# Half value products in 16-head attention units, and a GpSimd chain that begins one state later in a state-space pass

## What is computed

```
v = (x @ Wv.T).reshape(B, S, H, dk).transpose(0, 2, 1, 3)
...
scores = jnp.einsum('bhqd,bhkd->bhqk', q, k) / jnp.sqrt(jnp.float32(dk))
```

```
dt = jax.nn.softplus(jnp.einsum('blr,dr->bld', dt, dt_w) + dt_b)
...
dA = jnp.exp(dt[..., None] * A)
dBx = dt[..., None] * Bc[:, :, None, :] * xs[..., None]
def step(h, inp):
    h = dA_t * h + dBx_t
    y = jnp.einsum('bds,bs->bd', h, C_t)
```

## Time and profile before

| | before |
|---|---|
| median of 3 runs (lowest, highest) | 7721.05 us (7704.44, 7728.39) |
| profiled execution, its own time | 7713.37 us |
| its span, granted TensorE clock | 7711.6 us, 0.942 |
| PE busy | 6731.2 us, 87% |
| DVE busy | 5364.4 us, 70% |
| ACT busy | 4156.1 us, 54% |
| POOL busy | 2878.0 us, 37% |
| a0, c0, f2, c3: time of a unit | 10.5, 9.67, 9.4, 9.67 us |
| a1: time of a unit | 7.62 us, or 9.1 with a fall of the clock |
| m1 and m2: time of a group | 58.6 to 63 us |

### The profile page before, as it was taken

One profiled execution on the slowest core, in us unless ns is written; L12 is line 12 of the kernel. 1 busy time (PEld: TensorE's weight loads), 2 busy tenths in 40 slices (PEclk: granted clock), 3 DMA queues, 4 the chain that ended last, 5 costly groups with the idle time before them and its releaser, 6 DMA issues. The chain is left out here.

```text
span 7711.6 us, 190413 instructions
## 1 busy us (share of the span) xinstructions
PE 6731.2 (87%) x75040; PEld 4112.0 (53%) x75040; DVE 5364.4 (70%) x8861; ACT 4156.1 (54%) x6107; POOL 2878.0 (37%) x1663
## 2 busy tenths in 40 slices
PE   7989994877777899988898868989889999989898
PEld 5766683443442333333333335667557666767676
DVE  7867465454536999988999954668667777767544
ACT  4555333454535777767777764546444444446433
POOL 3311163332312888867888810136112221211000
PEclk9999996999978999998999989999999999999999
DMA  0000001000001222212222200000000000000000
GB/s 27 0 18 14 2 0 17 2 3 2 3 8 35 71 72 76 75 54 75 71 71 77 72 9 16 11 7 0 3 29 2 2 2 2 2 13 14 14 0 22
DMA packets 117005, 191.55 MB, mean 25 GB/s; under 512 B 39542, under 2 KB 75420, under 8 KB 116060
## 3 DMA queue, kind: packets, MB, share of 16 engines
q1 hardware_dynamic: 116572, 185.25, 7.6%
HBM read 174.99 MB, written 8.09 MB: 24 GB/s over the span
## 5 line engine op out<-in xcount | busy, mean ns | idle before, releaser
L2461 POOL TENSOR_TENSOR m_dBx<-m_dtx,m_Bs 128x1024 f32<-128x1024 f32 x518 | 1212.0, 2357 | 212.3 <-DVE m_hs L2798 170.0
L2798 DVE TENSOR_TENSOR_SCAN m_hs<-m_ps_dA,m_dBx 128x512 f32<-128x512 f32 x1036 | 1207.0, 1206 | 84.0 <-POOL m_dBx L2461 82.1
L2577 PE MATMUL m_ps_y<-m_yc,ident 128*128 128x512 f32 x2072 | 1068.3, 640 | 0.0
L2670 ACT ACTIVATE m_ps_dA<-m_dt,m_A 128x504 f32<-128x504 f32 x1036 | 687.0, 678 | 485.0 <-DVE m_hs L2798 482.3
L1998 POOL TENSOR_TENSOR a_s<-a_s,a_den 128x1024 f32<-128x1024 f32 x128 | 243.7, 1904 | 1141.7 <-DVE a_den L2044 1141.7
L2809 DVE TENSOR_TENSOR m_yc<-m_hs,m_ps_C 128x1024 f32<-128x1024 f32 x518 | 619.9, 1197 | 5.5 <-PE m_ps_C L2560 4.5
L2577 PEld LDWEIGHTS m_ps_y<-m_yc,ident 128*128 128x128 f32 x2072 | 361.7, 194 | 374.0 <-issue 374.0
L2560 PE MATMUL m_ps_C<-m_parts,m_sel 48*128 48x512 bf16 x520 | 205.3, 395 | 198.7 <-DVE m_yc L2809 198.5
L2560 PEld LDWEIGHTS m_ps_C<-m_parts,m_sel 48*128 48x128 bf16 x520 | 48.3, 93 | 608.2 <-DVE m_yc L2809 442.2
L580 POOL TENSOR_TENSOR c_kbd<-c_kf,c_hmask 128x1024 f32<-128x1024 f32 x66 | 125.1, 1895 | 527.5 <-ACT c_kf L493 514.6
L2042 DVE TENSOR_REDUCE a_den<-a_s 128x16 f32<-128x1024 f32 x128 | 156.1, 1219 | 206.7 <-ACT a_s L1950 206.7
(11 more groups left out here) (745 smaller groups left out, 16442.0 us busy)
## 6 DMA issues: line engine op xcount, KB each, us to landing
m_Bs<-m_BC_rows SPq DMA_DIRECT2D x260, 512.0 KB, 3.6
c_kvb<-in_ctxT SPq DMA_DIRECT2D x68, 128.0 KB, 2.1
c_kvb<-in_ctxT SPq DMA_DIRECT2D x17, 256.0 KB, 2.7
out_dram<-X SPq DMA_DIRECT2D x1, 4096.0 KB
m_BC_rows<-m_low SPq DMA_DIRECT2D x34, 64.0 KB, 2.8
m_part_rows<-m_split SPq DMA_DIRECT2D x34, 48.0 KB, 1.7
m_parts<-m_part_rows SPq DMA_DIRECT2D x34, 48.0 KB, 1.7
m_piece<-m_BC_rows SPq DMA_DIRECT2D x34, 32.0 KB, 1.7
```

The lines of the kernel that those rows point to most:

```text
L2461: return nc.gpsimd.tensor_tensor(to, one, other, ALU.mult)
L2577: last = nc.tensor.matmul(ps_y[:, m, :], C.ident[:], of[:, m, :], start=s == 0, stop=s == NS - 1)
L2670: nc.scalar.activation(seqs(ps_dA[:, h % 3, :]), seqs(dt[:, par, m, :]), ACT.Exp, scale=A[:, m, s:s + 1]).then_inc(decay, 1)
L2798: nc.vector.tensor_tensor_scan(hs[:, s % HS, m, :], ps_dA[:, (2 * s + m) % 3, :], dBx[:, s % BX, m, :], 0.0, ALU.mult, ALU.add).then_inc(s ...
```

## The change

In the 16-head units the moving operand of the value product becomes `wv_of(e)`: the 64 columns of the heads of one parity, read in runs of 8 columns with a step of 16. Half e of the partitions gets only those, `ps_b` is filled in 256 instead of 512 columns, and the copy of DVE reads them in one piece. Numbers of products, weight loads and copies stay.

In `mamba` the first piece of GpSimd's `front` (dt = x + ln) moves from behind dBx of state 11 to behind dBx of state 12, directly ahead of v += e.

```
+HV = NB * HD
...
+        wv_of = lambda e: wv[:].rearrange("p (n e d) -> p e n d", n=NB, e=2)[:, e, :, :]
...
                 for s in range(USEQ):
                     for b in range(2):
-                        last = nc.tensor.matmul(ps_b[S * b:S * b + S, s * D:(s + 1) * D], kvb[:, par, s * S:(s + 1) * S], wv[:],
-                                                start=True, stop=True)
+                        last = nc.tensor.matmul(ps_b[S * b:S * b + S, s * HV:(s + 1) * HV], kvb[:, par, s * S:(s + 1) * S],
+                                                wv_of(b), start=True, stop=True)
...
                     last = nc.vector.tensor_copy(vbd[r, par, :, :, e, 0:HD],
-                                                 ps_b[r, :].rearrange("p (s n e d) -> p s n e d", s=USEQ, n=NB, e=2)[:, :, :, e, :])
+                                                 ps_b[r, 0:USEQ * HV].rearrange("p (s n d) -> p s n d", s=USEQ, n=NB))
```

The same edits stand in `attn16_linear` (`xnT` in the place of `kvb`, and a copy that adds the bias). In `mamba`:

```
             def front(j, s, par):
-                if s == 11:
+                if s == 12:
                     pool.wait_ge(ln_ready, j + 1)
                     hold()
                     nc.gpsimd.tensor_tensor(dt[:, par, :, :], x[:], ln[:], ALU.add)
-                elif s == 12:
                     pool.wait_ge(excess, j + 1)
                     hold()
                     nc.gpsimd.tensor_tensor(v[:], v[:], e[:], ALU.add)
...
-            for s in range(11, 16):
+            for s in range(12, 16):
                 front(0, s, 0)
```

More of the change, by code:

```diff
@@ L884, in values @@
                     for e in range(2):
-                        last = nc.tensor.matmul(ps_b[S * e:S * e + S, s * D:(s + 1) * D], xnT[:, par, s * S:(s + 1) * S], wv[:],
-                                                start=True, stop=True)
+                        last = nc.tensor.matmul(ps_b[S * e:S * e + S, s * HV:(s + 1) * HV], xnT[:, par, s * S:(s + 1) * S],
+                                                wv_of(e), start=True, stop=True)
                 last.then_inc(v_done, 1)
@@ L1089, in diagonal_values @@
                     r = slice(S * e, S * e + S)
-                    own = ps_b[r, :].rearrange("p (s n e d) -> p s n e d", s=USEQ, n=NB, e=2)[:, :, :, e, :]
+                    own = ps_b[r, 0:USEQ * HV].rearrange("p (s n d) -> p s n d", s=USEQ, n=NB)
                     bias = bv[r, :].rearrange("p (n e d) -> p n e d", n=NB, e=2)[:, :, e, :]
```

## The result

The changed kernel takes 7737.85 us in the median of six runs (7735.14 to 7751.02), the kernel before 7707.62 in six (7699.78 to 7728.39). The ratio is 1.0039, 95% interval 1.0028 to 1.0049: slower, by 22 to 38 us, where +33 was forecast against a base that proved 9 us too high. The profiled execution took 7735.14 us with a span of 7733.4, 21.8 more than the span before.

| stretch | before, us | after, us | difference | forecast |
|---|---|---|---|---|
| start to the first scores of a1 (a0 and c0 with it) | 946.93 | 938.75 | -8.2 | -7.5 |
| a1, first to last scores | 261.88 | 242.69 | -19.2 | -23 |
| x1, f1 up to the first dt = x + ln of m1 | 1251.42 | 1246.64 | -4.8 | 0 |
| m1 and m2, first to last dt = x + ln | 1983.29 | 2042.73 | +59.4 | +71 |
| the rest (the attention of f2, and c3, with it) | 3268.08 | 3262.59 | -5.5 | -7.5 |

A forecast was written before the change was run, and what follows sets the result against it. PE was taken to bound a1, DVE m1 and m2, with the table stages like a1 but held by ACT's copy. The terms +71 - 13 - 10 - 15 = +33 us on a base of 7717 gave 7750 us, range 7705 to 7790.

The forecast's parts named there:

- the state-space pass: m1 and m2: two split steps on DVE held by POOL in each group, +71 us, bounds +63 and +79.
- dBx of state 12 comes ahead of the split and holds the first cast: m1 and m2, every group: dBx starts 0.85 us before the first cast; scan 9 starts 1.27 later than with one block.
- t0: State-space pass: the start of the split's first cast on DVE, 2863.63 in the one-block group of the trace before.
- Period 61.86: State-space pass: each group takes 60.34 + 1.27 us plus a surplus of 0.25, in all 61.86 us.
- The surplus of 0.25 a group: State-space pass: a longer hold adds something beyond its length, taken as 0.25 us, bounds 0 and 0.5.
- The mixture 14, 17 and 1: State-space loops before the change: of 32 splits, 14 are clean, 17 have one block and 1 has two.
- rival B: State-space pass: the blocks don't add up; -4 us there, 7675 in all; with no block, -34 and 7645. Chance 0.11.
- Table stages -15: Value products in a0, c0, f2, c3: ACT's last copy limits the gain to 0.12 us a unit, -15 us.
- Value products 0.43 us shorter: 16-head units: 64 columns at 31 ns a record make the batch 0.50 us, 0.43 less; in a1 -13 us.
- Half of the clock falls gone in a1: a1: of 13 PE clock falls at 1.5 us each, half vanish, -10 us, bounds -19.5 and +26.
- D: 16-head units: the strided products are no shorter, so only +71 remains, 7788 us. Chance 0.08.
- C: Table stages: PE's clock falls there too, in every third unit, 80 us, 7830 in all. Chance 0.06.

The follow-up runs named there:

- One block by design: The changed kernel with the split moved between the scan of state 7 and the weighing of state 6: 7701.47 us in one run.

## Why the prediction was right

The sign, the size and the mechanism held; the term that decided, the state-space pass, was +59 where +71 was said. By the medians the total is +30 for +33, nearer than its largest term; in the two profiled executions it is +22, so that nearness is luck.

- *dBx of state 12 comes ahead of the split and holds the first cast, dt = x + ln follows at once and holds the first subtraction.* Shown in every group. Scan 9 starts at t0 + 4.54 (forecast 4.71), with dBx of state 12 at t0 - 1.04 (forecast -0.85), since the weighing before the split, and with it t0, came 0.19 later. Counted from the start of scan 8 the forecast was 8.07 and the measured time is 8.09.
- *Period 61.86.* Measured 61.66. The surplus of 0.25 a group was the mis-sized term: it was read off the one group with two blocks, which is the first of its loop and has 0.3 more also in the changed kernel (61.99). Without it the period is 61.61 and the sum +63, which is 8 of the 12 us. One block by design and two in the changed kernel show that such a hold costs its length and nothing more. The other 3 to 4: the sum counted 32 groups, but only 30 periods lie between the first and the last dt = x + ln, 15 in each pass. They grew by 31.6 us in m1 and 29.3 in m2; the stretches ahead of the two loops and between the passes got 1.5 shorter.
- *The mixture 14, 17 and 1.* It set what there was to lose. The counts hold, but one reading behind them doesn't: in a clean group the split does not end before POOL starts. The last cast starts within 0.01 us of dt = x + ln in all 14 clean groups, and within 0.02 us in 7 of the 17 with one block (in the other 10 it comes 0.19 to 0.29 later). Beside the two starts of the earlier trace rows, 2745.82 and 2804.42:

```profile
2745.83 0.20 DVE L2788 CAST m_split<-m_rest 128x64 bf16<-128x64 f32 x1
2804.43 2.39 DVE L2788 CAST m_split<-m_rest 128x64 bf16<-128x64 f32 x1
```

  In the first the cast won and POOL's instruction took 2.41 us, in the second POOL won with 2.34. So two thirds of the groups of before are a tie that either engine can win. With the split early all groups are clean, and the pass takes 1944.0 us in the profile in place of 1983.3: -39, where rival B without any block had -34.
- *Table stages -15.* 0.11 to 0.12 us a unit in all four, bound by ACT's copy as said, though the idle time that this leaves on PE was taken as some 0.4 and is 0.14.
- *Value products 0.43 us shorter.* 0.41 in a1 (1.02 to 0.61): 38 ns a record in place of 31, which matters only there. By the Trainium skill ("TensorE: Matmul & The Clock Gate", Part 2, LDWEIGHTS) 64 columns take an estimated 53 ns to load; the rows have 38 with 64 columns moving and 31 with 18, so for these products the measurement decides against it. It is not so everywhere in this kernel. The weighing of a1 has loads of the same shape, with 18 columns moving and a granted clock of 1.00, at 50 ns each (64 in 3.19 us):

```profile
1086.16 3.19 PEld L913 LDWEIGHTS a_ps_c<-a_vbd,a_s 128*64 128x64 f32 x64
```

  In the code the products at 31 and 38 ns change the half of the output partitions from one to the next, and these stay on one half for eight in a row. Whether that is the reason no run tests; the 31 ns of the earlier trace rows was the nearer neighbour of the value products, but one of two.
- *Half of the clock falls gone in a1.* Behind the third unit 6 are left of 12 (7 of 13 with the third), by luck as much as by reason: no row told the way. a1 gained 19.2 from first to last scores, 23 was said; in the other runs with half products it takes 236.0 to 241.4 us, 20 to 26 under before's 261.9.
- *Rivals.* D fell with the 38 ns, C with the granted clock inside the table stages, 0.99 or 1.00 before and after. B fell in the changed kernel, since two instructions of POOL in a row do catch two steps.

The exclusion itself is what the Trainium skill's page "SBUF — State Buffer", "Who interferes with whom", states: a cast in a two-port mode, or a VectorE operation with both inputs in SBUF, needs ports that GpSimd reads through, and in the two-port modes the first to issue keeps them for the whole instruction. The rows agree: cast 1.38 and 2.20, subtraction 2.25 and 2.28 us, each let go within 0.1 us of the end of POOL's instruction. Scans and weighings with one input in PSUM keep their length beside POOL (2.33 and 1.2 us).

## What to carry to other kernels

Short steps on VectorE that exclude GpSimd belong where GpSimd waits for something that cannot come sooner; look for that gap in the trace, and remember that it is measured from events which the moved steps themselves delay. Two such steps caught by two GpSimd instructions in a row are held twice (here 3.2 us a group). The price is the whole time held where GpSimd's own chain waits for what is held (3.23 of 3.23, 2.0 of 2.0), and less where it doesn't (2.8 of 3.42). Where a reordering frees an engine and the time gets worse, take the collision away and measure again: here the later order is the better one as soon as the split is gone (57.1 against 58.4 to 60.2 us a group).

## What was not expected

- The order that cost 64 us is worth 1.4 us a group or more (2.1 in the mean) once the split is left out; before the last runs I took it for neutral.
- POOL lets single steps through between the scan's end and its own start: with 0.18 us of room, the first cast (0.16) and also the first subtraction (0.23, begun 0.02 us before POOL) ran, and the second cast was held.
- Halving the columns of a float32 product of 128x64 weights takes it from 64 to 38 ns a record in a row of 16 (1.02 to 0.61 us in a1), whether the 64 columns lie in one piece or in runs of 8.
- A fall of TensorE's clock in a1 comes 12 times behind the third unit at units of 7.62 us, 6 times at 7.21 and in one spell of four at 8.49.
